# One core: field pairs of a second-order interaction network grouped in three classes instead of two

## The reference

```python
x1 = einsum('bik,bjk,hij->bhk', e, e, W1) + b1     # W1 (128, 26, 26)
x2 = einsum('bik,bjk,hij->bhk', x1, e, W2) + b2    # W2 (128, 128, 26)
z = sum(concat([x1, x2], axis=1), axis=-1)          # (2048, 256)
h = relu(concat([z, dense_ctx]) @ W_top1 + b_top1)  # 272 -> 512
h = relu(h @ W_top2 + b_top2)                       # 512 -> 256
y = h @ W_top3                                      # 256 -> 1
```

## Time and profile before

| what | us |
| --- | --- |
| median of 3 runs | 604.69 (596.48 to 609.61) |
| profiled execution, its own time | 604.4 |
| its span, first to last instruction | 602.6 |
| mean granted TensorE clock in it | 0.952 of full speed |
| busy: PE, DVE, ACT, POOL | 523.6, 454.4, 256.9, 373.7 |

### The profile page before, as it was taken

How to read it: one execution, slowest core, us unless ns; L and a number is a source line. 1 busy time by engine, 2 the same in 40 slices (tenths; PEclk the granted TensorE clock), 3 DMA queues, 4 the chain that set the end, 5 groups by cost and what they waited for, 6 DMA issues and landing times.

```text
span 602.6 us, 13628 instructions
## 1 busy us (share of the span) xinstructions
PE 523.6 (87%) x5314; PEld 498.1 (83%) x5314; DVE 454.4 (75%) x1253; ACT 256.9 (43%) x528; POOL 373.7 (62%) x275
## 2 busy tenths in 40 slices
PE   4846986975979989898889898988999789999997
PEld 4524975965979989898889898988989689999987
DVE  6626965949777979697787969595959697996762
ACT  6513762543433535253535262433435253535501
POOL 5774687258735868677676878685858765740100
PEclk9966997996979999998999999998999899999999
DMA  6640022021312141303030213222231303000000
GB/s 194 160 62 8 5 29 36 7 48 22 41 27 33 17 47 16 46 11 47 9 46 12 40 20 36 24 30 29 23 36 16 43 9 44 11 9 1 2 1 2
DMA packets 30925, 19.58 MB, mean 32 GB/s; under 512 B 5171, under 2 KB 30326, under 8 KB 30761
## 3 DMA queue, kind: packets, MB, share of 16 engines
q0 software_dynamic: 8512, 4.38, 10.7%
q1 hardware_dynamic: 22377, 14.73, 9.9%
HBM read 19.08 MB, written 0.01 MB: 32 GB/s over the span
## 4 chain that ended last, share of the span: by engine, by line
PE 83%; issue 7%; ACT 3%; DVE 3%; another core or an unknown queue 2%; DMA 1%; SPq 0%; ACTq 0%; DVEq 0%
PE psum L858 34%; PE psum L878 19%; PE psum L895 11%; PE psum L938 4%; PE psum L916 4%; PE psum L872 3%; PE psum L811 3%; ACT v L699 2%; PE psum L834 1%; PE psum L832 1%; DVE work L624 1%; DMA t_area<-in_L_rec_W 1%; PE psum L804 1%; PE psum L828 1%
## 5 line engine op out<-in xcount | busy, mean ns | idle before, releaser
L377 POOL DMA_INDIRECT emb<-in_tbl,idx x266 | 371.0, 1395 | 162.8 <-issue 76.4
L858 PE MATMUL psum<-diag,work 128*109 128x108 f32 x2048 | 222.2, 266 | 22.2 <-issue 9.1
L858 PEld LDWEIGHTS psum<-diag,work 128*109 128x109 f32 x2048 | 210.6, 180 | 29.2 <-issue 14.7
L728 ACT COPY t_area<-psum 109x432 f32<-109x432 f32 x256 | 130.4, 519 | 193.1 <-PE psum L858 177.4
L624 DVE TENSOR_TENSOR work<-embT 128x32 f32<-128x32 f32 (+12 forms) x416 | 129.2, 387 | 0.0
L895 PE MATMUL psum<-table_parts,onehot 125*128 125x96 bf16 x1350 | 72.7, 213 | 22.5 <-issue 12.4
L895 PEld LDWEIGHTS psum<-table_parts,onehot 125*128 125x128 bf16 x1350 | 66.2, 102 | 27.8 <-issue 22.9
L878 PE MATMUL psum<-t_area,v 128*128 128x128 f32 x608 | 73.0, 277 | 5.3 <-issue 5.3
L878 PEld LDWEIGHTS psum<-t_area,v 128*128 128x128 f32 x608 | 70.5, 193 | 6.4 <-issue 6.3
L712 ACT COPY diag<-embT 32x416 f32<-32x416 f32 x128 | 69.9, 546 | 10.4 <-DVE embT L608 8.8
L454 DVE TENSOR_SCALAR onehot<-ids_left 125x1280 bf16<-125x1280 bf16 (+1 forms) x150 | 57.3, 453 | 0.5
(11 more groups left out here) (103 smaller groups left out, 467.6 us busy)
## 6 DMA issues: line engine op xcount, KB each, us to landing
ids_all<-in_short_ids SPq DMA_DIRECT2D x15, 625.0 KB
emb<-in_tbl,idx POOLq DMA_INDIRECT x266
t_area<-in_L_rec_W SPq DMA_DIRECT2D x1, 1664.0 KB
work<-in_W_top SPq DMA_DIRECT2D x2, 512.0 KB
onehot<-in_tbl SPq DMA_DIRECT2D x5, 156.2 KB
onehot<-in_tbl SPq DMA_DIRECT2D x5, 125.0 KB
t_area<-in_L_rec_W SPq DMA_DIRECT2D x1, 338.0 KB, 3.2
idx<-in_ids SPq DMA_DIRECT2D x4, 52.0 KB, 1.9
```

The source lines that it names most:

```text
L377: eng.indirect_dma_start(emb[n][:, f * K:(f + 1) * K], None, tables[f], bass.IndirectOffsetOnAxis(ap=idx[:, t * F + f:t * F + f + 1], axis=0),
L728: nc.scalar.copy(dst, src).then_inc(t_out, 1)
L858: last = nc.tensor.matmul(dst[:, :, c * TS:(c + 1) * TS], pairs[:, half, g % HALF, c, :], diag[:, g, :, :], start=True, stop=True)
```

## The change

The fields are three classes of 9, 9 and 8 (A, B, C). Pairs within a class (45 + 45 + 36 = 126, and a one: 127 columns) meet all 26 fields and the one. Pairs of a field of A with one of B (81 columns, the 18 fields of A and B from column 96, ones in the gaps: 127 columns as well) meet only the eight fields of C and the one. So a group has one matmul with 108 moving columns and one with 36, and 27 + 9 = 36 slots. A unit is 127 x 288. `pack` is four copies of 18 rows that bring eight cross slots into `crosses` (two slots of 128 rows); no other packing. `cin` has 34 matmuls for the second half of z and four for the first.

In the preparation the products of W2 and W1 are 53 matmuls in 13 bank jobs, the coefficients ten bank jobs (one of sums, seven "self", two "abc") with 12 copies on ACT; all of them stand ahead of tile 0. `gather(1)` is paced by one job a transfer instead of two. The first half of the raw short tables and the top weights lie elsewhere.

```diff
+LO, HI = [0, 9, 18], [9, 18, 26]
+BIG, CLASSES = 9, 3
+SELF = sum(tri(size) for size in SIZE)
+CONST = SELF
+ROWS = CONST + 1
+AB = SIZE[0] * SIZE[1]
...
             def pack(t, n):
-                into = packs
...
                 eng.wait_ge(t_out, UNITS * t + UNITS)
-                for c in range(2):
...
+                for q in range(QUADS):
+                    last = nc.vector.tensor_copy(crosses[K * q:K * q + LINEAR, n, :, :],
+                                                 tsum[FIELD0:FIELD0 + LINEAR, n, AB_C + CROSS * q:AB_C + CROSS * (q + 1), :])
+                last.then_inc(crosses_ready, 1)
...
             def make_pairs(t, n):
-                    nc.vector.tensor_copy(pairs[:, half, :, 0, FIELD0:ROWS], e[:, g, 0:HF])
-                    for r in range(HF):
...
+                    nc.vector.tensor_copy(pairs[:, half, :, 1, FIELD0:FIELD0 + LINEAR], e[:, g, 0:LINEAR])
+                    nc.vector.tensor_tensor(pairs[:, half, :, 1, 0:AB].rearrange("p g (b a) -> p g b a", a=SIZE[0]),
...
+                    for r in range(BIG):
...
             def unit_out(t, n, u):
-                    eng.wait_ge(packs_ready, t - 1)
-                src = psum[0:ROWS, u % T_BANKS, 0:columns * 2 * TS].rearrange("p (b s) -> p s b", b=columns)
+                src = psum[0:ROWS, u % T_BANKS, 0:columns * TS].rearrange("p (b s) -> p s b", b=columns)
...
+            sums_out()
             eng.wait_ge(consts_ready, 1)
-            eng.wait_ge(v_zero, 1)
-            v_out(AFTER_MOVED, AFTER_V0)
+            v_out(("self",))
+            eng.wait_ge(top2_ready, 1)
+            v_out(("abc",))
             for half in range(2):
                 fill_diag(0, 0, half)
-            v_out(AFTER_V0, AFTER_V1)
...
-                        for c in range(2):
-                            last = nc.tensor.matmul(dst[:, :, c * TS:(c + 1) * TS], pairs[:, half, g % HALF, c, :],
-                                                    diag[:, g, :, :], start=True, stop=True)
+                        nc.tensor.matmul(dst[:, :, 0:AB_C], pairs[:, half, g % HALF, 0, :], diag[:, g, :, :],
+                                         start=True, stop=True)
+                        last = nc.tensor.matmul(dst[:, :, AB_C:TS], pairs[:, half, g % HALF, 1, :], diag[:, g, :, LO[2]:F + 1],
+                                                start=True, stop=True)
...
             def cin(t, n):
-                eng.wait_ge(packs_ready, t + 1)
+                eng.wait_ge(t_out, UNITS * t + UNITS)
...
+                terms = [(V_SELF + m, m, ROWS) for m in range(F)] + [(V_ABC + c, AB_C + c, AB) for c in range(SIZE[2])]
...
+                eng.wait_ge(crosses_ready, t + 1)
+                for a in range(CROSS):
...
-            make_v(AFTER_MOVED, AFTER_V1)
+            make_sums()
+            make_v()
             for half in range(2):
                 t_units(0, 0, half)
-            make_v(AFTER_V1, PREPS)
```

387 lines of the change are left out of this document (185 added, 202 removed).

## The result

The changed kernel took 706.03 us (median of 4 executions, 700.06 to 708.14) against 602.77 us for the kernel before (median of 4): ratio 1.174, 95% interval 1.160 to 1.187. It is slower, by far more than the 2% that a measurement can tell, and outside the range of 586 to 628 us. The profiled execution took 708.14 us, with a span of 706.3.

A forecast was written before the change was run, and what follows sets the result against it. TensorE (PE) was taken as the bound, 27.3 us of matmuls in each 32 us tile. From 604.4 us: -24 preparation, +28.8 field products, +6.8 contraction, -9 waits = 607 us, range 586 to 628.

The forecast's parts named there:

- rival D: Field products: thinner streaming drops the clock to 1.2 GHz, +4.4 us a tile, 673 us; chance 0.05.
- its sign of being wrong: Steady tiles: a granted clock under 0.9 there would show the forecast wrong.
- Field products 110.8 ns a record: L858: load of 127 stationary columns sets the pace for both shapes, up from 95.8 ns, +1.92 us a tile.
- Contraction at 111.6: Contraction: 38 matmuls instead of 36, 111.6 ns a record, +0.45 us a tile.
- Rival A: Field products: only moving columns count, so they fall by 4.4 us a tile, 512 us; chance 0.05.
- DVE under 370 us and nobody faster for it: DVE: packing and pair work gets lighter, busy below 370 us, worth nothing on PE's path.
- ACT's copy 0.37 us: Moments out on ACT: the copy of 127 x 288 elements takes 0.37 us instead of 519 ns.
- The waits, -0.6 us a tile: PE waiting for ACT's copies while `ids_all` lands: -0.6 us a tile, bounds 0 and -1.3.
- tile 0 at 59.5 forecast: Preparation: fewer copies let tile 0 begin at 59.5 us, before 73.1; 52 or 66 depending on the slow stretch.
- Tile 1 at 90: Start of tile 1 after tile 0, its lookups and contraction: 90 us, before 114.0.
- the gain of 24 us: Preparation and tile 0: earlier start of tile 1, 24 us gained, bounds 16 and 33.
- Rival C: Preparation: the ramp gives nothing, tile 0 at 76 and tile 1 at 106 us, 16 us later, 623; chance 0.14.

The follow-up runs named there:

- e14: Changed kernel, second matmul moving 108 columns, and 12 ACT copies a tile holding up the first lookups in tiles 2 to 14: 707.62 us, ratio 1.155 to kernel before.
- e13: Changed kernel, with 12 small ACT copies a tile that the first part of the lookups waits for in tiles 2 to 14: 770.17 us, ratio 1.256 to kernel before.
- e8: Kernel before with the pacing of the gathers taken away: 526.58 us, ratio 0.997 to the kernel before.
- e9: Changed kernel unedited, run again on a chip without gaps: 561.97 us, ratio 1.056 to the kernel before.
- e4: Changed kernel with a single transfer of the short tables' ids, tiles 2 to 15 reusing those of tile 1: 723.29 us, ratio 1.177 to kernel before.
- e1: Changed kernel, second matmul of each group moving all 108 columns instead of 36 and issued first: 673.61 us, ratio 1.094 to kernel before.
- e2: Changed kernel, second matmul of each group moving 72 columns instead of 36 and issued first: 703.13 and 717.36 us, beside 618.94 for the kernel before.
- e16: Changed kernel with table gathers retimed to keep clear of the lookups (nine ahead from tile 4 on), on a chip with gaps: 719.17 us (two executions).
- e12: Kernel before with the pacing of the gathers taken away, on another chip without gaps: 528.30 us, ratio 0.990 to kernel before.
- e17: Changed kernel without the table gathers of tiles 2 to 15, id transfers kept: 561.93 us, ratio 1.055 to kernel before.
- e18: Changed kernel with gathers retimed: two ahead of the first lookups, six between the parts, eight behind the second: 568.05 us, ratio 1.069 to kernel before.
- e11: Changed kernel, second matmul moving 108 columns and gathers retimed away from the lookups, on a chip without gaps: 561.46 us, ratio 1.054 to kernel before.
- e15: Kernel before, with 12 small ACT copies a tile that the first lookups wait for in tiles 2 to 14: 680.51 us, ratio 1.107.

## Why the prediction was wrong

**The step that failed** is rival D, in its condition, its price and its chance (0.05). It had the right suspicion: half the streaming, and the clock. It asked only whether the clock would fall in the field products, and "nothing in the trace shows" that was taken as a reason to let it be. The right question was what happens after the next fall, for the kernel before had falls already (0.98 in the steady tiles): with full field products they pass in a few us, with thin ones they last until something dense comes. In the sum the clock stood at nothing; its sign of being wrong, a granted clock under 0.9 in the steady part, is what came (0.82). On price: I gave the 36-column record 111 ns at the low clock and the other 180. A record takes 215 in the mean, with 36 columns in the second matmul or with 108 (311.34 in the kernel after, 390.10 in e14): what limits the pace there, the load by my own reading, slows down with the clock. A whole tile of field products at the low clock costs 128 x 104 ns = 13.3 us more, where I had 4.4, and by the clock of 0.82 some third of a tile's time was spent there.

The Trainium skill (TensorE: Matmul & The Clock Gate, "HAM oscillation — how this bites in real kernels") describes a kernel whose repeated waits bring the clock down in each round. The trace agrees that waiting comes before the fall (at 306.9 us, inside the gap), though each wait here is only about 1 us. In that section the wait alone is the cause; e14 and e13, with equal drips and 62.6 us apart, show that what is streamed afterwards decides what a fall costs.

**The sum, where the 89.4 us of the ten tiles went** (409.1 against 319.7 us; the profiled executions are 103.7 us apart, 708.14 and 604.4, the start of tile 1 gives -0.4 of it and the other tiles the remaining 14.7). Take e8 and e9 as the same work without gaps or falls, though they ran on two chips: 275.1 and 296.9. The work differs by 21.8 us. PE idles 40.1 us after against 25.6 before: 14.5. The rest, 53 us, is PE busy for longer: 369.0 - 296.9 = 72.1 after, 294.1 - 274.8 = 19.3 before. That last part I put down to the clock, with small waits hidden in the busy time.

**Point by point.**
- Field products 110.8 ns a record: right, 110 ns above. Alike the shapes are only in the mean: behind the 108-column pair the next start comes after 0.28 us, behind the 36-column pair after 0.16 (324.03, 324.31, 324.47). Contraction at 111.6: right (68 records in 7.59 us, e.g. from 331.56 on in the chain). Together +1.92 + 0.45 = 2.37 us a tile forecast; e9 against e8 gives (296.9 - 275.1)/10 = 2.18. Rival A, with 61 ns in the mean, is refuted.
- DVE under 370 us and nobody faster for it: right (344.9). ACT's copy 0.37 us: 0.40.
- The waits, -0.6 us a tile: wrong in sign and place. Those behind ACT did go, but by the profile before they were 3.6 us in its ten tiles, not the larger part of 4.7 us a tile, and the lookups' idle time rose from 11 to 34 us in ten tiles. I had named `ids_all` as the cause of starvation; e4 shows that it is not. In the earlier trace rows I chose a stretch of 42 lookups without a gap, and I did not look at the 48 of the first part.
- Preparation: tile 0 at 59.5 forecast, 56.6 measured: right in this execution, and in part by luck. In the changed kernel's other profiles on chips with gaps it began at 55.5 to 58.1 us (e1, e2, e13) or at 69.3 to 72.8 (e4, e14, e16), where the kernel before has 73.1; why it is the one or the other is open. Tile 1 at 90, measured 113.6: the gain of 24 us was lost again on the way. Tile 0 took 26.2 us at the low clock (56.60 to 82.79) instead of 14.2, and its lookups 21.8 instead of 5.5 (to 104.60); the one-hot, for which I had 2.3 us of waiting, was in time. -2.9 + 12.0 - 2.3 + 16.3 + 0.5 for the contraction = 23.6. Rival C had a loss of this size (16 us), in another place.
- On chips without gaps the gain does not exist at all: tile 0 begins at 52.9 us in e12, the kernel before but for its gathers, and at 52.7 in e9. Without it and without the waits my sum is +28.8 + 6.8 = +35.6 us. Measured there: +30.0 (e9) and +29.0 (e17, without gathers). That is near in part by luck: some 6 us of the 30 are tile 0 at the low clock, which the sum does not have (tile 1 begins at 93.4 us in e9 and at 87.6 in e12). The 2.18 us a tile are the better test.

So the counted costs were right within a tenth for a tile, and both gains that I set against them came from disturbances that one set of runs has and another has not. The change was slower wherever it ran: by 5.6% where PE was fed, by 17% where it was not.

**What stays open.** Why PE's lookups starve on some chips is not settled, and the gathers' part in it is not shown. For it: in the kept profiles with gaps (before, after, e1 to e4, e16) 23 stretches of lookups have no gather beside them, and none of them has a gap; of the 101 first parts and tile 1 lookups with gathers beside them 86 have one. And there is the pair of e13 and e16 (24.5 against 5.9 us). Against it: that pair differs in time too; in the kernel before the 90 lookups at 100.09 us ran without a gap with four gathers beside them, and 58 of e14 did; and of 79 second parts with gathers beside them only 8 have a gap. Whether clearing the steady tiles of gathers would bring their clock back was not measured, since e17 and e18 met chips without gaps. Why the changed kernel's gaps are three times as long is open as well: in the ten tiles the kernel before had two to four gathers beside its first parts, against five or six, but a longer stretch meets more gathers, so this may be effect and not cause. No version beats the kernel before: the one that streams more (e1, e11) brings the changed kernel from a ratio of 1.174 to 1.094 where there are gaps and costs nothing where there are none, but stays above it. e8 and e12 cannot be told from it.

## What to carry to other kernels

Of a thinner matmul ask not only what it costs at full clock but how the kernel recovers from the falls that it already has. Where a load limits the pace anyway, more moving columns cost almost nothing (298.1 against 296.9 us for ten tiles), and they can be what brings the clock back (e1 against the changed kernel, e14 against e13). And a gain that consists of less waiting should be priced at nothing unless the wait's releaser is known: two terms of this sum rested on waits (those of the preparation and those behind ACT's copies), and neither survived the change of chip.

## What the runs showed of the hardware

- Sets of runs on different chips differ in how PE is fed. The same kernel took 532 to 534 us in three of them and 603 to 624 in the three others. What the profiles show of the difference is "issue" gaps in the densest instruction stream (42.6 ns a lookup) with the falls of the clock behind them, and idle time in the preparation.
- At the low clock float32 records with 127 stationary columns take 215 ns in the mean, with 108 and 36 moving columns by turns (after) as with 108 in both (e14); at full clock 110 in either case.
- Once the clock was down, field products at 108 + 36 columns did not bring it back, though PE was busy: 27.3 us of tile 0 in e9 (0.50), 26 us of it after (0.52), 10.8 us of tile 6 (0.50). At 108 + 108 columns 4 to 6 us did (e1, e14, e15). At 108 + 72 (e2) it stayed low for 10.3 us of tile 6 (0.50). The 256 columns of `layer1` and the dense lookups did bring it back.
- A gather that took seven microseconds (290.20) had nine others behind it, which then ran beside the lookups. The Trainium skill (SBUF — State Buffer, "SBUF: two separate sides") tells of DVE copies that hold GpSimd back from writing descriptors. The row is long, 7.07 us against 0.95, and may be such a case; but in that time DVE made products, with a single copy of 0.30 us among them (291.74), so the page's case is not quite this one, and no run tells which it is.
